# Head 0 of an attention block takes its row tiles in another order, with every engine's queue in that head written out

## The chip, the cores and the metric

The kernel runs on one core of a Trainium2 chip. The metric is the device time of one execution in microseconds; lower is better.

## What is computed

One block over x of 1024 tokens by 256 channels: a layer norm, then 16 heads of causal attention with 128 dimensions each and a small quantised linear layer beside them, both added to x. Cut to what matters:

```python
xn = _layernorm(x)
q, k, v = (xn @ Wq), (xn @ Wk), (xn @ Wv)            # 16 heads of 128
q, k = rmsnorm(q, q_rms_w), rmsnorm(k, k_rms_w)
scores = q k^T / sqrt(128) - distance * slope[head]   # causal
y = rmsnorm(softmax(scores) @ v, subln_w)
x = x + y @ Wproj + quantise_fp8(xn / s) @ (w8 * ws) * s
```

## The kernel before

The kernel is written engine by engine: each of the blocks for SyncE, GpSimd, TensorE, ScalarE and VectorE is one queue in a fixed order, and semaphores tie them together. `over_heads` (L220) calls each engine's `head(h, ...)` for heads 0 and 1 with plain numbers, for 2 to 13 in a loop, and again with numbers for 14 and 15. What is matrix work is done in three products: every float32 operand is split into a rounded high part and a low part, and `product` (L505) multiplies high by high, low by high and high by low.

The 1024 tokens are eight row tiles of 128; two neighbours are a pair (0 to 3). For each head and tile, `project` (L543) makes q, k and v of one tile as six products of 384 columns into one PSUM bank, `copy_qkv` (L772) moves them on ScalarE to a place that `stage_of` names, `square_qk` squares a pair, `mean_squares` (VectorE) sums it, `norm_qk` (GpSimd, L399) takes the reciprocal root and scales q and k with `scale_qk` (L231). In head 0 VectorE scales instead (`norm_first`). `transpose_qk` turns a pair, `qk_hi` (ScalarE) and `qk_lo` (VectorE) split it, `split_v` (GpSimd) splits v.

A row tile i of a head then goes through `score` (i + 1 tiles of 128 keys), `mask` (VectorE adds the bias and takes the row maximum), `exps` (ScalarE), `transpose_probs` (TensorE), `probs_hi` (ScalarE) and `probs_lo` (VectorE). The order of the row tiles is ORDER = 7, 0, 6, 1, 5, 2, 4, 3 in every head. `attend` sums the first four tiles (group 0) in the head itself and the other four in the next. The projections of head h + 1 lie between the row tiles of head h. So in head 0 the queues also hold head 1's projections, norms and transposes, the weights of head 2 (`split_w`) and VectorE's decoding of the 8-bit weights in eight steps (`decode_w8`), which end in `wb_ready`.

Ahead of head 0 lie the loads, the layer norm, 24 warm-up products of TensorE, the transposes of the normalised x (four calls, each waiting for four tiles), ten more warm-ups, the eight projections of head 0 and two of head 1, and the transposes of head 0's q and k. The places for copied projections are two buffers in turn, except for pairs 2 and 3 of head 0, which use halves of `bias` and `probs`. A copy into a used place waits for the norm and the v split of the pair before.

## Time and profile before

| | us |
|---|---|
| median of 3 runs | 534.56 |
| lowest and highest | 532.73 to 536.16 |
| the profiled execution | 534.62 |
| its span, first to last instruction | 532.6 |
| TensorE busy | 512.6 |
| VectorE busy | 436.2 |
| ScalarE busy | 376.9 |
| GpSimd busy | 344.4 |

The times of an engine are from one profiled execution. Matmuls are pipelined, so the next one starts before the one ahead ends: the difference of two starts is what a matmul costs in a row of its kind, and its own duration is what a reader of its result waits. "Idle before" is the time in which the engine did nothing, with the instruction that ended it.

### The profile page before, as it was taken

To read this page: it belongs to the slowest core of one execution; us is meant where nothing else is said; L and a number is where in the kernel's file an instruction comes from. 1 tells how busy PE (TensorE), PEld (TensorE's weight loads), DVE (VectorE), ACT (ScalarE), POOL (GpSimd) and SP (SyncE) were. 2 spreads that over 40 slices of the span, in tenths; PEclk is the share of its full clock that TensorE was granted. 3 is DMA by queue.
4 is the path that set the end of the run, shared out by engine and by line. 5 is a ranking of instruction groups with operands and counts; after the bars stand their busy time and mean duration, and the time that the engine had idled before them with its cause. 6 is when DMAs were issued, how large, how long until landed. Compare 5 with 4: busy or idle time off the path is not lost. (4 is left out here: it accounts for less than half of the span.)

```text
span 532.6 us, 11964 instructions
## 1 busy us (share of the span) xinstructions
PE 512.6 (96%) x3348; PEld 467.0 (88%) x3348; DVE 436.2 (82%) x1061; ACT 376.9 (71%) x887; POOL 344.4 (65%) x491
## 2 busy tenths in 40 slices
PE   8869899999999999999999999999999999999886
PEld 3858699999989999998999999899999999999775
DVE  5768788888898888888888888988888897988973
ACT  2658568676876878677687868678786767869550
POOL 4658387684858668584877848585785848567121
PEclk9999899999999999999999999999999999999998
DMA  5200100001010100101010010101001000000002
GB/s 153 70 1 2 39 1 22 20 2 41 2 40 0 33 7 0 39 0 39 0 39 0 0 39 0 39 0 39 0 0 39 0 10 0 11 1 1 2 0 79
DMA packets 18614, 10.82 MB, mean 20 GB/s; under 512 B 2208, under 2 KB 18592, under 8 KB 18592
## 3 DMA queue, kind: packets, MB, share of 16 engines
q1 hardware_dynamic: 17600, 10.49, 6.7%
q8 instruction: 10, 0.16, 0.1%
q10 hardware_dynamic: 992, 0.07, 0.1%
q14 instruction: 12, 0.10, 0.1%
HBM read 9.51 MB, written 1.05 MB: 20 GB/s over the span
## 5 line engine op out<-in xcount | busy, mean ns | idle before, releaser
L781 ACT ACTIVATE stage<-qkv_ps 128x384 f32<-128x384 f32 x119 | 58.6, 492 | 88.6 <-PE qkv_ps L509 88.6
L973 DVE TENSOR_TENSOR pT_lo<-pT_ps,pT_hi 128x384 fp32r<-128x384 f32 (+1 forms) x192 | 100.6, 552 | 16.0 <-ACT pT_hi L809 15.9
L809 ACT ACTIVATE pT_hi<-pT_ps 128x384 fp32r<-128x384 f32 (+1 forms) x192 | 86.5, 485 | 31.0 <-PE pT_ps L588 31.0
L801 ACT ACTIVATE probs<-probs,neg_max 128x1024 f32<-128x1024 f32 (+7 forms) x128 | 99.1, 775 | 8.4 <-DVE neg_max L964 7.7
L588 PE MATMUL pT_ps<-ident,probs 128*128 128x128 f32 x576 | 86.2, 277 | 5.6 <-ACT probs L801 4.7
L507 PE MATMUL qkv_ps<-w_hi,xT_hi 128*128 128x384 f32 x242 | 87.2, 360 | 0.7 <-DVE xT_lo L1050 0.7
L588 PEld LDWEIGHTS pT_ps<-ident,probs 128*128 128x128 f32 x576 | 66.7, 141 | 18.0 <-ACT probs L801 6.7
L509 PE MATMUL qkv_ps<-w_hi,xT_lo 128*128 128x384 f32 x242 | 81.5, 337 | 0.0
L508 PE MATMUL qkv_ps<-w_lo,xT_hi 128*128 128x384 f32 x242 | 81.3, 336 | 0.0
L403 POOL TENSOR_TENSOR qk_r<-qk_ms,minus_half 128x4 f32<-128x4 f32 x64 | 65.4, 1022 | 21.2 <-DVE qk_ms L938 19.5
L507 PE MATMUL yT_ps<-pT_hi,v_hi 128*128 128x256 f32 (+1 forms) x224 | 73.7, 329 | 0.4 <-DVE pT_lo L973 0.4
L509 PE MATMUL yT_ps<-pT_hi,v_lo 128*128 128x256 f32 (+1 forms) x224 | 72.5, 324 | 0.0
L508 PE MATMUL yT_ps<-pT_lo,v_hi 128*128 128x256 f32 (+1 forms) x224 | 72.3, 323 | 0.0
L964 DVE CUSTOM_DVE_ANT_0 probs<-score_big,bias 128x1024 f32<-128x1024 f32 (+1 forms) x64 | 64.9, 1013 | 2.3 <-PE score_big L509 2.3
L233 POOL TENSOR_TENSOR qk_n<-stage,qk_r 128x512 f32<-128x512 f32 x60 | 62.4, 1040 | 5.7 <-POOL qk_r L403 1.9
L507 PE MATMUL score_big<-kT_hi,qT_hi 128*128 128x512 f32 (+2 forms) x128 | 50.9, 398 | 3.9 <-DVE kT_lo L947 3.9
L935 DVE TENSOR_REDUCE qk_ms<-squares 128x4 f32<-128x512 f32 x62 | 42.4, 683 | 14.1 <-ACT squares L788 13.0
L420 POOL TENSOR_TENSOR v_lo<-stage,v_hi 128x256 fp32r<-128x256 f32 x62 | 46.0, 741 | 9.4 <-POOL v_hi L417 0.5
L507 PEld LDWEIGHTS qkv_ps<-w_hi,xT_hi 128*128 128x128 f32 x242 | 45.9, 190 | 3.6 <-ACT stage L781 2.2
L443 POOL TENSOR_TENSOR y_r<-y_ms,minus_half 128x4 f32<-128x4 f32 x32 | 32.7, 1021 | 22.7 <-DVE y_ms L999 14.9
L508 PEld LDWEIGHTS qkv_ps<-w_lo,xT_hi 128*128 128x128 f32 x242 | 45.7, 189 | 0.0
L509 PE MATMUL score_big<-kT_hi,qT_lo 128*128 128x512 f32 (+2 forms) x128 | 45.6, 356 | 0.0
...
## 6 DMA issues: line engine op xcount, KB each, us to landing
...
q_col<-in_q_w ACTq DMA_DIRECT2D x1, 0.5 KB, 3.0
```

What stands on the lines that cost most here:

```text
L233: eng.tensor_tensor(qk_n[:, k % 2], stage_of(h, k)[:, :, 0:2 * D].rearrange("p t (a d) -> p t a d", d=D), qk_r[:, k % 2, :].rearrange("p ( ...
L403: pool.tensor_tensor(qk_r[:, k % 2, :], qk_ms[:, k % 2, :], minus_half[:, 0:4], ALU.pow).then_inc(qk_r_ready, 1)
L420: pool.tensor_tensor(v_lo[:, par, 2 * k:2 * k + 2, :], v, v_hi[:, par, 2 * k:2 * k + 2, :].bitcast(f32), ALU.subtract).then_inc(v_split, 1)
L507: pe.matmul(dst, a_hi, b_hi, start=start, stop=False)
L508: pe.matmul(dst, a_hi, b_lo, start=False, stop=False)
L509: return pe.matmul(dst, a_lo, b_hi, start=False, stop=stop)
L588: last = pe.transpose(ps[:, (j - a) * P:(j - a + 1) * P], probs[:, s % 2, j * P:(j + 1) * P], ident[:, :])
L781: act.activation(stage_of(h, k // 2)[:, k % 2, :], qkv_bank(h, k)[:, 0:3 * D], ACT.Copy).then_inc(qkv_read, 1)
L801: act.activation(probs[:, s % 2, 0:(i + 1) * P], probs[:, s % 2, 0:(i + 1) * P], ACT.Exp, bias=neg_max[:, par, s:s + 1], scale=-1.0, accum ...
L809: act.activation(pT_hi[g][:, a:b, r * P:(r + 1) * P], pT_ps[(CHUNK0[s] + k) % 2][:, 0:(b - a) * P].rearrange("p (j t) -> p j t", t=P), ACT ...
L964: dve.tensor_tensor_reduce(out=probs[:, s % 2, 0:w], in0=ps[:, at:at + w], in1=bias[:, par, (NT - 1 - i) * P:(NT - 1 - i) * P + w], scale= ...
L973: dve.tensor_tensor(pT_lo[g][:, a:b, r * P:(r + 1) * P], pT_ps[(CHUNK0[s] + k) % 2][:, 0:(b - a) * P].rearrange("p (j t) -> p j t", t=P), ...
```

## The change

- **Order.** Head 0 takes its row tiles as 1, 7, 0, 6, 3, 5, 2, 4; all other heads keep ORDER. The first four are the same group. Row tile 1 is scored into the `misc` bank and needs pair 0 only; each score of head 0 waits for the low part of its own pair instead of for all four.
- **Places.** Pairs 2 to 5 (2 and 3 of head 0, 0 and 1 of head 1) get rooms of their own, in `bias_more` and `early_room`; the latter is shared with y_blocks, w8T, xqT, x_u, x_m and the statistics, which gives those two added waits (`part_y`, the copy of w8T). `probs` is no longer used for a projection, so the second mask of head 0 doesn't wait for the splits of v. Head 1's last projection goes to the other bank, and head 1's first transposes wait for all its copies.
- **Queues.** Every engine but SyncE has a `first_head` with the order in head 0 written out. Pairs 1 and 3 of head 0 are scaled on GpSimd, 0 and 2 on VectorE. The low part of head 0's weights is made on GpSimd instead of VectorE. GpSimd splits head 2's weights and most of v later, after head 1's first norm. TensorE transposes x tile by tile as tiles come, starts a projection when the first half of the contraction is there, and has two more of head 1's projections ahead of the first big score. The last decoding step is one of its own, and head 1's first score goes ahead of the transposes of the 8-bit weights.

The diff, cut to its core. The rest follows from it: `order(h)`, `chunks(h, s)` and `chunk0(h, s)` take the places of ORDER, CHUNKS and CHUNK0 everywhere, and `head` on each engine calls `first_head` and returns where h is 0.

```diff
     ORDER = [7, 0, 6, 1, 5, 2, 4, 3]
+    FIRST_ORDER = [1, 7, 0, 6, 3, 5, 2, 4]
     GROUPS = [sorted(ORDER[:4], reverse=True), sorted(ORDER[4:], reverse=True)]
     RANK = {i: (g, GROUPS[g].index(i)) for g in range(2) for i in GROUPS[g]}
-    CHUNKS = [[(j, min(j + 4, i + 1)) for j in range(0, i + 1, 4)] for i in ORDER]
-    CHUNK0 = [sum(len(c) for c in CHUNKS[:s]) for s in range(NT + 1)]
-    CPH = CHUNK0[NT]
+    def order(h):
+        return FIRST_ORDER if isinstance(h, int) and h == 0 else ORDER
+    def chunks(h, s):
+        i = order(h)[s]
+        return [(j, min(j + 4, i + 1)) for j in range(0, i + 1, 4)]
...
@@ -111,7 +124,11 @@
         yT_hi = sb("yT_hi", [P, 2, 4 * P], f32r)
         yT_lo = sb("yT_lo", [P, 2, 4 * P], f32r)
         y_sq = sb("y_sq", [P, 2, 4 * P])
-        y_blocks = sb("y_blocks", [P, 4 * P])
+        early_room = sb("early_room", [P, 12 * P])
+        y_blocks = early_room[:, 0:4 * P]
+        x_u, x_m = early_room[:, 4 * P:6 * P], early_room[:, 6 * P:8 * P]
+        w8T = early_room[:, 8 * P:10 * P].bitcast(bf16).rearrange("p (k c) -> p k c", k=KT)
+        xqT = early_room[:, 10 * P:11 * P].bitcast(bf16).rearrange("p (k t) -> p k t", k=KT)
         y_part = sb("y_part", [P, 16])
         y_pair = sb("y_pair", [P, 4, 2, 4], f32r)
...
@@ -255,9 +269,10 @@
         def stage_of(h, k):
-            if isinstance(h, int) and h == 0 and k >= 2:
-                room = bias[:, 1, :] if k == 2 else probs[:, 1, :]
-                return room[:, 0:6 * D].rearrange("p (t n) -> p t n", t=2)
+            if isinstance(h, int) and 2 <= NPAIR * h + k < 6:
+                if h == 0:
+                    return bias_more[:, T + (k - 2) * 6 * D:T + (k - 1) * 6 * D].rearrange("p (t n) -> p t n", t=2)
+                return early_room[:, k * 6 * D:(k + 1) * 6 * D].rearrange("p (t n) -> p t n", t=2)
             return stage[:, k % 2]
...
@@ -289,9 +304,11 @@
         def is_last(h):
             return isinstance(h, int) and h == H - 1
-        def score_at(i):
+        def score_at(h, i):
             w = (i + 1) * P
+            if isinstance(h, int) and h == 0 and i == 1:
+                return misc, 0, [(0, w)]
...
             for n in range(2):
                 at = slice(n * NT // 2, (n + 1) * NT // 2)
+                if n == 1:
+                    pool.wait_ge(w_hi_done, 1)
+                    pool.tensor_tensor(w_lo[:, 0], w_raw[:, 0], w_hi[:, 0].bitcast(f32), ALU.subtract).then_inc(w_split, 1)
                 pool.wait_ge(var_ready, n + 1)
                 pool.tensor_tensor(rstd[:, at], rstd[:, at], minus_half[:, at], ALU.pow).then_inc(rstd_ready, 1)
...
+                if isinstance(h, int) and h == 0 and k not in POOL_NORMS:
                     return
                 pool.wait_ge(qk_r_ready, n + 1)
+                if isinstance(h, int) and n <= NPAIR:
+                    past(pool, qk_normed, n)
                 past(pool, qkT_ready, n - 1)
                 scale_qk(pool, h, k)
...
@@ -459,16 +481,36 @@
             split_w(1, 1)
             norm_qk(0, 0)
             norm_qk(0, 1)
-            split_v(0, 0, 0)
             norm_qk(0, 2)
             norm_qk(0, 3)
-            for k in (1, 2, 3):
-                split_v(0, 0, k)
+            split_v(0, 0, 0)
+            split_v(0, 0, 1)
+            norm_qk(1, 0)
             pool.wait_ge(small_loaded, 80)
             pool.wait_ge(xT_read, 2 * KT)
+            split_v(0, 0, 2)
+            split_v(0, 0, 3)
+            split_w(2, 0)
+            def first_head():
+                split_v(1, 1, 0)
+                norm_qk(1, 1)
+                norm_qk(1, 2)
+                norm_qk(1, 3)
+                split_wp(0, 0)
+                split_v(1, 1, 1)
+                split_v(1, 1, 2)
+                split_v(1, 1, 3)
+                pool.wait_ge(ffn_scaled, 1)
+                clip_x(0)
             def head(h, par, tile, after):
                 first, last = isinstance(h, int) and h == 0, is_last(h)
+                if first:
...
-                past(pe, qkv_read, NT * h + k - (1 if isinstance(h, int) and (h == 0 or h == 1 and 1 <= k <= 6) else 0))
+                past(pe, qkv_read, NT * h + k - (1 if isinstance(h, int) and h <= 1 else 0))
                 if k == 0 and not (isinstance(h, int) and h <= 1):
                     pe.wait_ge(misc_read, misc_done(h - 2, "proj1a" if not (isinstance(h, int) and h == 2) else "qkT2"))
                 for kt in range(KT):
+                    if isinstance(h, int) and h == 0 and k % 4 == 0:
+                        pe.wait_ge(xT_read, KT * (k // 4) + kt + 1)
...
-                i, n = ORDER[s], NT * h + s
-                if s == 0:
+                i, n = order(h)[s], NT * h + s
+                if isinstance(h, int) and h == 0:
+                    pe.wait_ge(misc_read, misc_done(-1, f"qkT{i // 2}"))
+                elif s == 0:
                     pe.wait_ge(misc_read, misc_done(h - 1, "qkT3"))
-                past(pe, scores_masked, n - 1)
-                ps, at, parts = score_at(i)
+                past(pe, scores_masked, n if isinstance(h, int) and (h, s) == (1, 0) else n - 1)
+                ps, at, parts = score_at(h, i)
...
-            def transpose_x(n):
-                half, kt = n // KT, n % KT
-                pe.wait_ge(xn_ready, 4 * half + 4)
+            def transpose_x(half):
                 for t in range(4):
-                    last = pe.transpose(xT_bank(n)[:, t * P:(t + 1) * P],
-                                        bias_xn(4 * half + t)[:, kt * P:(kt + 1) * P], ident[:, :])
-                last.then_inc(xT_ready, 1)
+                    pe.wait_ge(xn_ready, 4 * half + t + 1)
+                    for kt in range(KT):
+                        last = pe.transpose(xT_bank(half * KT + kt)[:, t * P:(t + 1) * P],
+                                            bias_xn(4 * half + t)[:, kt * P:(kt + 1) * P], ident[:, :])
+                        if t == 3:
+                            last.then_inc(xT_ready, 1)
             transpose_x(0)
+            warm(KEEP_WARM)
+            project(0, 0, 0)
+            project(0, 0, 1)
             transpose_x(1)
-            warm(KEEP_WARM)
-            for k in range(NT):
-                if k % 4 == 0:
-                    pe.wait_ge(xT_read, KT * (k // 4 + 1))
-                project(0, 0, k)
-                if k == 1:
-                    transpose_x(2)
-                    transpose_x(3)
-                if k == NT - 1:
-                    transpose_qk(0, 0, 0, -1)
-                    transpose_qk(0, 0, 1, -1)
+            project(0, 0, 2)
+            project(0, 0, 3)
+            project(0, 0, 4)
+            project(0, 0, 5)
+            project(0, 0, 6)
+            project(0, 0, 7)
             project(1, 1, 0)
+            transpose_qk(0, 0, 0, -1)
+            transpose_qk(0, 0, 1, -1)
+            project(1, 1, 1)
             transpose_qk(0, 0, 2, -1)
-            project(1, 1, 1)
+            score(0, 0, 0)
             transpose_qk(0, 0, 3, -1)
-            score(0, 0, 0)
             project(1, 1, 2)
+            project(1, 1, 3)
...
+            def first_head():
+                transpose_probs(0, 0)
+                score(0, 0, 1)
+                project(1, 1, 4)
+                project(1, 1, 5)
+                score(0, 0, 2)
+                score(0, 0, 3)
+                transpose_probs(0, 1)
+                project(1, 1, 6)
+                score(0, 0, 4)
+                transpose_probs(0, 2)
+                score(0, 0, 5)
+                transpose_probs(0, 3)
+                project(1, 1, 7)
+                transpose_qk(1, 1, 0, 0)
+                transpose_probs(0, 4)
+                score(0, 0, 6)
+                score(0, 0, 7)
+                transpose_probs(0, 5)
+                transpose_qk(1, 1, 1, 0)
+                transpose_qk(1, 1, 2, 0)
+                attend(0, 0, 0, 0)
+                transpose_probs(0, 6)
+                transpose_qk(1, 1, 3, 0)
+                attend(0, 0, 0, 1)
+                transpose_probs(0, 7)
+                score(1, 1, 0)
+                transpose_w8()
...
                 act.wait_ge(qkv_ready, n + 1)
-                if k % 2 == 0 and not (isinstance(h, int) and h == 0):
-                    last = k // 2 + 1 if isinstance(h, int) and h == 1 and k <= 2 else pair - 1
+                if k % 2 == 0 and not (isinstance(h, int) and pair < 6):
+                    last = pair - 5 if isinstance(h, int) and h == 1 else pair - 1
...
@@ -847,26 +930,72 @@
             round_xT(0)
             round_xT(1)
-            for k in range(NT):
-                copy_qkv(0, k)
-                if k == 1:
-                    round_xT(2)
-                    round_xT(3)
-                if k % 2:
-                    square_qk(0, k // 2)
             act.wait_ge(const_ready, 3)
+            make_bias(0, 0)
+            copy_qkv(0, 0)
+            copy_qkv(0, 1)
+            round_xT(2)
+            round_xT(3)
+            copy_qkv(0, 2)
+            square_qk(0, 0)
+            copy_qkv(0, 3)
+            copy_qkv(0, 4)
+            square_qk(0, 1)
+            copy_qkv(0, 5)
+            copy_qkv(0, 6)
+            square_qk(0, 2)
+            copy_qkv(0, 7)
+            square_qk(0, 3)
             act.wait_ge(wq_col_ready, 1)
-            for k in range(NPAIR):
-                qk_hi(0, 0, k)
-                if k == 1:
-                    copy_qkv(1, 0)
-                    make_bias(0, 0)
-                if k == 2:
-                    copy_qkv(1, 1)
+            qk_hi(0, 0, 0)
+            copy_qkv(1, 0)
+            copy_qkv(1, 1)
+            qk_hi(0, 0, 1)
+            qk_hi(0, 0, 2)
             square_qk(1, 0)
+            qk_hi(0, 0, 3)
+            exps(0, 0, 0)
+            probs_hi(0, 0)
+            copy_qkv(1, 2)
+            copy_qkv(1, 3)
+            def first_head():
+                copy_qkv(1, 4)
+                exps(0, 0, 1)
+                square_qk(1, 1)
+                probs_hi(0, 1)
+                exps(0, 0, 2)
+                copy_qkv(1, 5)
+                square_qk(1, 2)
+                probs_hi(0, 2)
+                exps(0, 0, 3)
+                copy_qkv(1, 6)
+                exps(0, 0, 4)
+                probs_hi(0, 3)
+                copy_qkv(1, 7)
+                square_qk(1, 3)
+                qk_hi(1, 1, 0)
+                probs_hi(0, 4)
+                exps(0, 0, 5)
+                exps(0, 0, 6)
+                probs_hi(0, 5)
+                qk_hi(1, 1, 1)
+                make_bias(1, 1)
+                exps(0, 0, 7)
+                probs_hi(0, 6)
+                qk_hi(1, 1, 2)
+                qk_hi(1, 1, 3)
+                act.wait_ge(wb_ready, 1)
+                square_y(0, 0)
+                y_hi(0, 0, 0)
             def head(h, par, tile, after):
                 first, last = isinstance(h, int) and h == 0, is_last(h)
+                if first:
+                    first_head()
...
@@ -1067,10 +1207,8 @@
             variances(0)
             normed(0)
             moments(1)
+            split_xT(0)
             variances(1)
-            split_xT(0)
-            dve.wait_ge(w_hi_done, 1)
-            dve.tensor_tensor(w_lo[:, 0], w_raw[:, 0], w_hi[:, 0].bitcast(f32), ALU.subtract).then_inc(w_split, 1)
             split_xT(1)
             normed(1)
...
+                if s == 7:
                     dve.scalar_tensor_tensor(wide, sign, 1.0, mag, ALU.add, ALU.mult).then_inc(wb_ready, 1)
             def norm_first(k):
                 dve.wait_ge(qk_r_ready, k + 1)
                 past(dve, qkT_ready, k - 1)
...
+                link(dve.reciprocal(ffn_s[:, 1:2], ffn_s[:, 0:1]))
+                dve.tensor_tensor(ffn_s[:, 3:4], ffn_s[:, 0:1], ffn_s[:, 2:3], ALU.mult).then_inc(ffn_scaled, 1)
             mean_squares(0, 0)
             mean_squares(0, 1)
             norm_first(0)
             mean_squares(0, 2)
-            norm_first(1)
             mean_squares(0, 3)
+            norm_first(2)
             qk_lo(0, 0, 0)
-            norm_first(2)
-            norm_first(3)
             qk_lo(0, 0, 1)
             qk_lo(0, 0, 2)
+            mask(0, 0, 0)
             qk_lo(0, 0, 3)
-            mask(0, 0, 0)
+            mean_squares(1, 0)
             def add_ffn(h, t):
...
+            def first_head():
+                decode_w8(0)
+                decode_w8(1)
+                mask(0, 0, 1)
+                decode_w8(2)
+                decode_w8(3)
+                probs_lo(0, 0)
+                mean_squares(1, 1)
+                mask(0, 0, 2)
+                mask(0, 0, 3)
+                probs_lo(0, 1)
+                decode_w8(4)
+                probs_lo(0, 2)
+                mask(0, 0, 4)
+                mean_squares(1, 2)
+                decode_w8(5)
+                probs_lo(0, 3)
+                mask(0, 0, 5)
+                mask(0, 0, 6)
+                mean_squares(1, 3)
+                probs_lo(0, 4)
+                qk_lo(1, 1, 0)
+                scale_ffn()
+                mask(0, 0, 7)
+                probs_lo(0, 5)
+                qk_lo(1, 1, 1)
+                decode_w8(6)
+                probs_lo(0, 6)
+                decode_w8(7)
+                qk_lo(1, 1, 2)
+                qk_lo(1, 1, 3)
+                y_lo(0, 0)
+                probs_lo(0, 7)
+                mask(1, 1, 0)
```

## Rows read from the trace of the kernel before

**Rows 1.** TensorE and the others by stretches: stretch, length, busy us (instructions), then granted clock (PEclk).

```profile
0.00:62.00 62.00, 50.89 (x282) 40.65 (x283) 43.60 (x111) 35.45 (x78) 37.16 (x67) 0.97 0.20 57
62.00:94.00 32.00, 31.93 (x216) 29.44 (x215) 26.23 (x64) 24.32 (x57) 23.01 (x32) 1.00 0.06 17
```

**Rows 2.** Waits of TensorE, 0 to 62 us: total, times, longest

```profile
PE score_big L507 <- DVE kT_lo L947: 3.9, 2, 2.2
PE pT_ps L588 <- ACT probs L801: 2.8, 2, 1.9
...
PE score_small L564 <- DVE qk_n L233: 0.8, 1, 0.8
...
PE score_big L564 <- DVE qk_n L233: 0.6, 1, 0.6
```

**Rows 3.** The same, 62 to 503 us

```profile
PE pT_ps L588 <- ACT probs L801: 0.8, 1, 0.8
```

**Rows 4.** The view by stretches again, around two stops of TensorE

```profile
32.00:36.00 4.00, 2.14 (x14) 1.92 (x13) 2.24 (x5) 1.51 (x4) 2.66 (x3) 1.00 0.01 4
58.00:59.00 1.00, 0.60 (x2) 0.51 (x3) 1.00 (x4) 0.83 (x3) 0.00 (x0) 0.74 0.83 239
59.00:60.00 1.00, 1.00 (x4) 0.81 (x3) 0.74 (x2) 0.00 (x0) 0.00 (x0) 0.50 0.12 34
...
61.00:62.00 1.00, 1.00 (x7) 0.87 (x6) 0.00 (x0) 0.00 (x0) 0.00 (x0) 0.56 0.00 0
```

**Rows 5.** Timeline of TensorE: start, busy us, line, operation, count, idle before

```profile
11.02 2.32 PE L651 MATMUL score_big<-ident_b 128*128 128x512 bf16 x10
14.08 0.45 PE L507 MATMUL qkv_ps<-w_hi,xT_hi 128*128 128x384 f32 x1 [0.74 <-DVE xT_lo L1050]
...
15.24 0.33 PE L507 MATMUL yT_ps<-w_hi,xT_hi 128*128 128x384 f32 x1
...
16.28 0.60 PE L662 MATMUL misc<-ident,bias 128*128 128x128 f32 x4
...
30.94 0.50 PE L507 MATMUL score_big<-kT_hi,qT_hi 128*128 128x512 f32 x1 [1.69 <-DVE kT_lo L947]
...
35.78 1.09 PE L588 MATMUL pT_ps<-ident,probs 128*128 128x128 f32 x8 [1.86 <-ACT probs L801]
...
58.40 0.75 PE L507 MATMUL score_big<-kT_hi,qT_hi 128*128 128x512 f32 x1 [2.18 <-DVE kT_lo L947]
...
62.48 0.39 PE L507 MATMUL qkv_ps<-w_hi,xT_hi 128*128 128x384 f32 x1
```

**Rows 6.** Timeline of GpSimd

```profile
16.35 1.83 POOL L382 TENSOR_TENSOR w_lo<-w_raw,w_hi 128x768 fp32r<-128x768 f32 x1
...
21.59 1.39 POOL L403 TENSOR_TENSOR qk_r<-qk_ms,minus_half 128x4 f32<-128x4 f32 x1 [0.88 <-DVE qk_ms L938]
...
25.83 1.01 POOL L403 TENSOR_TENSOR qk_r<-qk_ms,minus_half 128x4 f32<-128x4 f32 x1 [0.21 <-DVE qk_ms L938]
...
41.90 1.04 POOL L233 TENSOR_TENSOR qk_n<-stage,qk_r 128x512 f32<-128x512 f32 x1
```

**Rows 7.** Timeline of VectorE

```profile
12.48 0.95 DVE L1073 TENSOR_TENSOR w_lo<-w_raw,w_hi 128x768 fp32r<-128x768 f32 x1
...
21.42 0.69 DVE L233 TENSOR_TENSOR qk_n<-stage,qk_r 128x512 f32<-128x512 f32 x1
...
23.50 1.25 DVE L233 TENSOR_TENSOR qk_n<-stage,qk_r 128x512 f32<-128x512 f32 x1
...
33.22 1.23 DVE L964 CUSTOM_DVE_ANT_0 probs<-score_big,bias 128x1024 f32<-128x1024 f32 x1 [2.33 <-PE score_big L509]
...
55.73 1.00 DVE L1113 TENSOR_TENSOR y_sq<-y_sq,wb 128x512 f32<-128x512 f32 x1
56.77 0.85 DVE L1114 SCALAR_TENSOR_TENSOR wb<-y_sq 128x512 bf16<-128x512 f32 x1
```

**Rows 8.** Timeline of ScalarE

```profile
15.43 0.49 ACT L781 ACTIVATE stage<-qkv_ps 128x384 f32<-128x384 f32 x1 [3.56 <-PE qkv_ps L509]
```

108 lines of the change are left out of this document (67 added, 41 removed).

## The prediction, made before the changed kernel ran

> **What bounds the kernel now.** I read the busy time by stretches first. From 62 us to 94 us TensorE is busy 31.93 of 32 us, in the first 62 us only 50.89 [rows 1]. The waits of TensorE say the same for the rest: between 62 and 503 us its largest wait is 0.8 us [rows 3]. So heads 1 to 14 are a solid block of matmuls and only the two ends have air. The change touches head 0 and the projections of head 1, all of it before TensorE begins head 2's first projection, and nothing behind that point runs in another order. The question is therefore one number: when does that projection start? Before, it starts at 62.48 us [rows 5], and whatever it moves forward the end moves forward too, as long as head 1 stays a solid block.
>
> In front of it the reader is to see three losses.
> - The start: TensorE's first real product begins at 14.08 us [rows 5].
> - Stops after that: 3.9 us for k's low part (kT_lo) in two stops, 2.8 us for probabilities in two, 0.8 and 0.6 us for normalised q and k [rows 2]. The sum is 8.1 us.
> - A slow stretch: before the score at 58.40 TensorE waits for kT_lo (the longest stop on its list of waits, 2.2 us [rows 2]), and then the granted clock is 0.74, 0.50 (twice) and 0.56 in the four microseconds from 58 to 62 [rows 4], that is 1.2 GHz for most of them. Lost: 0.26 + 0.50 + 0.50 + 0.44 = 1.7 us.
>
> From 14.08 to 62.48 are 48.4 us; less 8.1 and 1.7 this leaves 38.6 us of work. That is the same work after the change: 16 projections, 8 + 8 groups of transposes, nine score tiles (and head 1's second), the 36 tiles of probabilities, one half attention. As a cross-check: six matmuls of 384 columns take 16.28 - 15.24 = 1.04 us, so 0.173 us each, or 0.45 ns a column, and eight transposes take 1.09 us with their drain of some 0.24, or 0.107 each [rows 5]. About 61,000 columns at 0.45 ns are 27.5 us, 76 transposes at 0.107 us are 8.1 us; the rest of the 38.6 us is the change between kinds and the drain at a stop.
>
> **The change part by part.**
>
> *The start.* The low part of head 0's weights goes from VectorE (0.95 us, at 12.48 [rows 7]) to GpSimd, where the same operation on head 1's weights takes 1.83 us [rows 6]. Its input is ready when ScalarE has rounded the high part, at 10.3 us, so it ends at about 12.2. On GpSimd the second reciprocal root is queued behind it; VectorE now asks for that at about 12.6, so the root waits for nothing and is merely 0.6 us later than before, while VectorE, which has lost 0.95 us of work, reaches the second normalisation at 13.8 against 13.95. VectorE's low part of x is now first needed for one half of the contraction only, and is there at 12.2; the second at 13.3. The transposes of x start at about 9.9 us when the 24 warm-up products end, finish at about 10.8, ten warm-ups (2.32 us [rows 5]) follow, and the first projection starts at 13.15 instead of 14.08. Gain 0.9 us. The bounds: 12.2, if the warm-ups were to end sooner (they don't depend on data), and 14.1, if the GpSimd subtraction took twice as long. The second group of transposes then starts right after two projections. Squares, sums and roots of the first three pairs come no earlier, though: ScalarE does each square one copy later than before, so these 0.9 us are not passed on to them.
>
> *The norms.* Pairs 1 and 3 are scaled on GpSimd for 1.04 us [rows 6] instead of on VectorE for 0.69 to 1.25 us [rows 7]. VectorE's queue gets shorter, GpSimd's longer by 2 us, and its order changes: the splits of v, head 2's weights (2.75 us) and the splits of head 1's v are put behind head 1's first norm. Walking the queues with these durations gives normalised pair 1 at 23.95, pair 2 at 25.8, pair 3 at 27.4. TensorE has eight projections done at 22.45, one of head 1's and the first two transposes at 24.4, another projection at 25.45. Then it stops 0.4 us for pair 2, 0.25 for the low part of pair 0 (the small score needs only this one, which is what the order 1, 7, 0, 6 brings) and 0.45 for pair 3: 1.1 us in place of 0.8 + 0.6 + 1.7 us.
>
> *The big score.* Row tile 7 is scored at about 30.25 instead of 30.94 [rows 5], but with two more projections (2.1 us), a small score and its transposes already done. The copies of these projections wait for no buffer, since pairs 2 to 5 have rooms of their own. While mask (1.23 us), exponentials (1.15 us and a read of the sum) run [rows 7, 8], TensorE has two projections and one short score in hand and 1.4 us of row tile 6: the stop of 1.86 us at 35.78 goes, and so does the next of 0.95 (together the 2.8 us of [rows 2]).
>
> *The middle of the head.* What is late next are the handovers between ScalarE and VectorE. The fourth set of transposes (row tile 6) needs exponentials that follow the copies of tile 0's transposes, which wait for VectorE behind the mask of tile 6: 0.45 us. Head 1's first transposes go into the bank of the projection just before them; they wait for its copy, 0.19 us after the last product and 0.49 us long [rows 8]: 0.75 us. The transposes of tile 5 wait for exponentials and then for the low part of tile 3: 0.4 + 0.4 us. Head 1's fourth transposes wait for the low parts of pair 1, which stand behind a mask and two low parts: 0.8 us.
>
> *The score of head 1.* It needs the low part of pair 3, behind the last two steps of the decoding (1.00 and 0.85 us [rows 7]), one low part of probabilities and pair 2's. With the gaps between instructions, after pair 1's low part, that is 1.05 + 0.45 + 0.85 + 2 x 0.75 = 3.85 us on VectorE, against 0.45 + 1.8 + 0.6 us on TensorE: a stop of 1.0 us instead of 2.2. The bounds are 0 and 2.2 us. I take 1.0; at that length no row shows a fall of the clock (the stop of 1.86 us ahead of 35.78 [rows 5] left it at 1.00 [rows 4]), so the 1.7 us of the slow stretch are saved whole.
>
> *Ports.* VectorE and GpSimd disturb each other. The root on GpSimd takes 1.39 us beside a VectorE product of two SBUF operands, and 1.01 us later on [rows 6]; the same VectorE product takes 0.69 us, and 1.25 beside a GpSimd subtraction [rows 7]. I have put 0.45 us for this into the three norm stops. The Trainium skill, SBUF — State Buffer, section "Who interferes with whom", says that the first to issue holds the shared pair for its whole instruction and the other blocks fully, and counts VectorE's two-port modes, such as the decoding's tensor_scalar steps, among those concerned. By that rule, GpSimd being busy without a break from 27 to 54 us, six decoding steps would wait up to 1 us each.
>
> *The rest* costs nothing: the bias made earlier lies in ScalarE's idle time while head 0 is projected; buffers that share room (w8T, xqT and the x tiles with pairs 4 and 5) are written only in head 1, and their added waits are for pairs that GpSimd has finished by 51 us; the loads of weights hang on splits that are not late.
>
> **The sum.** New start of head 2's first projection: 13.15 + 38.6 + stops of (1.1 + 0.45 + 0.75 + 0.8 + 0.8 + 1.0 = 4.9) = 56.65 us, against 62.48. Gain 5.8 us: 0.9 start, 3.2 stops, 1.7 clock. The queue walk itself, instruction by instruction, ended at 56.1, so 5.8 is the careful side. The profiled execution took 534.62 us beside a span of 532.6; the median of three is 534.56, so both are the same here: 534.6 - 5.8 = 528.8 us, with a span near 526.8.
>
> **Rivals.**
> 1. *The VectorE queue becomes the bound of head 0.* VectorE has hardly a pause there, in a fixed order in which decoding and sums stand between masks and low parts. If each of six decoding steps is held by GpSimd for 0.4 to 0.6 us (1.25 - 0.69 is 0.56 [rows 7]), 2.4 to 3.6 us come back into the stops and the gain is 2.2 to 3.4 us: about 531.8 us. For it: GpSimd has hardly a pause after 27 us. Against: most of this delay would have to fall on the steps TensorE waits for. This is also what the skill's rule of the shared port would give. Chance 0.23.
> 2. *The handovers hide better than walked.* If the stops in the middle overlap with slack that I count double (the walk's 56.1, or the 2 us of middle stops gone), the gain is 7 to 9 us: 526.6 us. Against: the decode-and-low-part chain ahead of head 1's score is serial. Chance 0.15.
> 3. *It does not shorten anything:* the stop before head 1's score stays over 2 us because normalised pair 3 of head 1 comes late from GpSimd (it waits for the transposes of pair 1), the clock drops as at 58.40 and the 1.7 us return: gain 5.8 - 1.2 - 1.7 = 2.9, or with rival 1 nothing. Time about 531.7 us, chance 0.11.
> 4. *Slower than before:* a fall of the clock early. The three norm stops at 25 to 28 us lie 1 us apart; if the chip answers them with 1.2 GHz until head 0 is through, 26 us, then at the half microsecond that each microsecond of it cost in [rows 4] 13 us are lost: 534.6 - 5.8 + 13 = 541.8 us. It eats the gain from 12 us of half clock on, and makes the kernel slower by over 1% from 22 us on. Against: before, stops of 0.8, 0.6, 1.69 and 1.86 us within 12 us left the clock at 1.00 [rows 2, 4, 5]. Chance 0.06.
>
> **How the numbers follow.** The forecast (gain 4.5 to 7) holds 0.45. A change under 1% (5.35 us) can't be told from none by a measurement of this kernel. The forecast's span is cut by that bound: of its 0.45, 0.35 lie above it. With rival 2 faster has 0.50; within 1% has 0.44, which is rivals 1 and 3 and the rest of the forecast; slower has rival 4's 0.06. The range of 8 in 10 reaches from rival 2's far end (gain 9) to a gain of 1.5: 525.6 to 533.0 us.
>
> **What would show it.** Right: first projection near 13.1; score of row tile 7 near 30.2 with four of head 1's projections behind it; stops after 13 us that sum to about 5 us, none of 2 us; granted clock 1.00 from 13 us on; head 2's first projection at 56 to 57; the rest as before. Wrong: a stop of over 2 us before head 1's score with a clock of 0.5 behind it; decoding steps on VectorE of 0.8 us and more; new waits of TensorE between 60 and 100 us, where head 1 would have to lose what head 0 gained.

## The result

The changed kernel takes 525.99 us (median of four, 525.42 to 526.85), the kernel before 534.92 beside it: ratio 0.9849, 95% interval 0.9818 to 0.9879. A second set of runs gave 526.79 us and a ratio of 0.9847 (0.9823 to 0.9872). The forecast was 528.8 us, range 525.6 to 533.0. The sign, the place and the three parts (start, stops, clock) were right; the gain is 8.9 us in the first set and 7.7 in the second, against 5.8.

The stretches of the profile of after (stretch, length, busy us with instructions, then granted clock), cut where head 2's first projection now starts:

```profile
0.00:54.68 54.68, 49.56 (x288) 39.59 (x288) 41.55 (x110) 36.09 (x79) 39.79 (x68) 1.00 0.23 65
54.68:86.68 32.00, 32.00 (x214) 29.88 (x214) 26.24 (x64) 23.74 (x56) 24.66 (x36) 1.00 0.06 18
```

Beside [rows 1]: the same 32 us of solid block follow, but from 54.68 us on instead of 62.48. TensorE's waits, first up to 60 us and then to 495 us (total, times, longest):

```profile
PE pT_ps L634 <- ACT probs L883: 0.7, 2, 0.4
PE yT_ps L608 <- ACT stage L863: 0.6, 1, 0.6
PE pT_ps L634 <- DVE pT_lo L1110: 0.5, 2, 0.3
PE misc L608 <- DVE kT_lo L1086: 0.4, 1, 0.4
...
PE score_big L549 <- DVE kT_lo L1086: 0.3, 1, 0.3
```

```profile
PE yT_ps L549 <- DVE pT_lo L1110: 0.4, 1, 0.4
```

The 8.1 us of [rows 2] in six stops have become 2.5 us in seven, none over 0.6; from 55 to 495 us there is hardly a wait, as in [rows 3]. The marks of the forecast in TensorE's timeline of after (start, busy us, operation, idle before):

```profile
9.01 1.41 PE L708 MATMUL pT_ps<-ident,bias 128*128 128x128 f32 x8 [0.39 <-DVE bias L1183]
10.26 2.32 PE L697 MATMUL score_big<-ident_b 128*128 128x512 bf16 x10
12.23 0.53 PE L549 MATMUL qkv_ps<-w_hi,xT_hi 128*128 128x384 f32 x1
...
24.92 0.34 PE L551 MATMUL yT_ps<-w_hi,xT_lo 128*128 128x384 f32 x1
25.39 0.66 PE L608 MATMUL score_big<-ident,qk_n 128*128 128x128 f32 x4
...
29.48 0.48 PE L549 MATMUL score_big<-kT_hi,qT_hi 128*128 128x512 f32 x1
...
40.99 0.34 PE L551 MATMUL yT_ps<-w_hi,xT_lo 128*128 128x384 f32 x1
41.91 0.66 PE L608 MATMUL yT_ps<-ident,qk_n 128*128 128x128 f32 x4 [0.58 <-ACT stage L863]
...
44.80 0.66 PE L634 MATMUL pT_ps<-ident,probs 128*128 128x128 f32 x4 [0.41 <-ACT probs L883]
45.72 0.44 PE L634 MATMUL pT_ps<-ident,probs 128*128 128x128 f32 x2 [0.26 <-DVE pT_lo L1110]
...
49.37 0.66 PE L608 MATMUL misc<-ident,qk_n 128*128 128x128 f32 x4 [0.44 <-DVE kT_lo L1086]
...
52.61 0.50 PE L549 MATMUL score_big<-kT_hi,qT_hi 128*128 128x512 f32 x1 [0.31 <-DVE kT_lo L1086]
...
54.68 0.39 PE L549 MATMUL qkv_ps<-w_hi,xT_hi 128*128 128x384 f32 x1
```

Against [rows 5]: the first projection starts at 12.23 instead of 14.08, the score of row tile 7 at 29.48 instead of 30.94 with four of head 1's projections done instead of two, head 1's first score at 52.61 instead of 58.40 and at full clock (its first product takes 0.50 us, not 0.75), head 2's first projection at 54.68.

So 7.8 us were won up to there in this pair of traces; the span fell by 8.8, from 532.6 to 523.8. The other 1.0 us can't be credited to the change. From head 2's first projection on TensorE runs the same 3061 products in both. All but the last sixty take 454.1 us in before and 454.7 in after, and between 453.8 and 455.1 in all fourteen traces, whatever the kernel. The last sixty take 11.1 us where the clock fell among them (before, twice, and one execution of after) and 9.5 us in the other eleven, 1.6 us less: near the end both kernels have the same stops, and the clock fell there in one execution and not in the other. Granted clock of before, of the same kernel profiled once more, and of after profiled once more:

```profile
520.00:521.00 1.00, 1.00 (x4) 0.72 (x3) 0.26 (x1) 0.00 (x0) 0.63 (x1) 0.50 0.00 0
```

```profile
59.00:60.00 1.00, 1.00 (x4) 0.74 (x3) 0.57 (x1) 0.00 (x0) 0.00 (x0) 0.50 0.00 0
...
520.00:521.00 1.00, 1.00 (x3) 0.74 (x3) 0.45 (x2) 0.00 (x0) 0.44 (x1) 0.50 0.00 0
```

```profile
512.00:513.00 1.00, 1.00 (x5) 0.90 (x5) 0.38 (x2) 0.00 (x0) 0.43 (x1) 0.57 0.00 0
513.00:514.00 1.00, 1.00 (x3) 0.72 (x3) 0.28 (x1) 0.00 (x0) 0.61 (x1) 0.50 0.00 0
```

### The profile page after: what moved, and what is told of

It is laid out like the page before. It is cut to its first block and busy times, and to the rows that moved or that the text cites. A ratio compares the mean times of both kernels' runs of the same rounds, so it can differ in the third digit from the quotient of the medians.

```text
span 523.8 us, 11974 instructions
## 1 busy us (share of the span) xinstructions
PE 509.9 (97%) x3348; PEld 465.2 (89%) x3348; DVE 433.6 (83%) x1058; ACT 377.3 (72%) x887; POOL 349.5 (67%) x494
## 3 DMA queue, kind: packets, MB, share of 16 engines
HBM read 9.51 MB, written 1.05 MB: 20 GB/s over the span
## 5 line engine op out<-in xcount | busy, mean ns | idle before, releaser
L863 ACT ACTIVATE stage<-qkv_ps 128x384 f32<-128x384 f32 x116 | 57.2, 493 | 88.1 <-PE qkv_ps L551 88.1
L1110 DVE TENSOR_TENSOR pT_lo<-pT_ps,pT_hi 128x384 fp32r<-128x384 f32 (+2 forms) x192 | 100.8, 552 | 11.9 <-ACT pT_hi L891 11.7
L891 ACT ACTIVATE pT_hi<-pT_ps 128x384 fp32r<-128x384 f32 (+2 forms) x192 | 86.8, 486 | 28.8 <-PE pT_ps L634 28.7
L883 ACT ACTIVATE probs<-probs,neg_max 128x256 f32<-128x256 f32 (+7 forms) x128 | 99.1, 776 | 3.2 <-DVE neg_max L1101 2.3
L1074 DVE TENSOR_REDUCE qk_ms<-squares 128x4 f32<-128x512 f32 x62 | 42.4, 684 | 13.5 <-ACT squares L870 13.5
L442 POOL TENSOR_TENSOR v_lo<-stage,v_hi 128x256 fp32r<-128x256 f32 x60 | 44.4, 739 | 8.7
```

The costliest lines, as they stand in the source:

```text
L442: pool.tensor_tensor(v_lo[:, par, 2 * k:2 * k + 2, :], v, v_hi[:, par, 2 * k:2 * k + 2, :].bitcast(f32), ALU.subtract).then_inc(v_split, 1)
L863: act.activation(stage_of(h, k // 2)[:, k % 2, :], qkv_bank(h, k)[:, 0:3 * D], ACT.Copy).then_inc(qkv_read, 1)
L883: act.activation(probs[:, s % 2, 0:(i + 1) * P], probs[:, s % 2, 0:(i + 1) * P], ACT.Exp, bias=neg_max[:, par, s:s + 1], scale=-1.0, accum ...
L891: act.activation(pT_hi[g][:, a:b, r * P:(r + 1) * P], pT_ps[(chunk0(h, s) + k) % 2][:, 0:(b - a) * P].rearrange("p (j t) -> p j t", t=P), ...
L1110: dve.tensor_tensor(pT_lo[g][:, a:b, r * P:(r + 1) * P], pT_ps[(chunk0(h, s) + k) % 2][:, 0:(b - a) * P].rearrange("p (j t) -> p j t", t=P ...
```

## The experiments

The ruler of most runs is the distance from TensorE's first projection to head 2's first projection, read from each trace, since everything the change does to the queues lies in it and the start is taken out. "At full clock" is this distance less half a microsecond for each microsecond at half clock in it; that takes the slow stretches as pure loss, which is an upper bound, because other engines catch up meanwhile. Each ratio is against executions of the kernel before made beside that run, whose medians were 534.92, 534.27, 533.65 and 534.45 us in the four sets, so it is the ratios that compare across rows, not the times.

| run | first projection | head 2's | distance | at full clock | time, us | ratio to before (95%) |
|---|---|---|---|---|---|---|
| before | 14.08 | 62.48 | 48.40 | 46.7 | 534.92 | |
| before, again | 13.90 | 62.32 | 48.42 | 46.7 | 535.81 (one) | |
| before, stop filled | 14.11 | 61.92 | 47.81 | 46.1 | 533.08 | 0.9976 (0.9957 to 0.9994) |
| before, new start | 12.34 | 61.20 | 48.86 | 47.2 | 532.62 | 0.9980 (0.9959 to 1.0001) |
| before, new order | 13.97 | 62.35 | 48.38 | 45.4 | 532.78 | 0.9963 (0.9946 to 0.9980) |
| before, new rooms | 13.93 | 62.98 | 49.05 | 46.1 | 534.07 | 0.9998 (0.9983 to 1.0012) |
| after | 12.23 | 54.68 | 42.45 | 42.4 | 525.99 | 0.9849 (0.9818 to 0.9879) |
| after, again | 12.71 | 54.95 | 42.24 | 42.2 | 526.79 | 0.9847 (0.9823 to 0.9872) |
| after, old start | 13.94 | 56.05 | 42.11 | 42.1 | 527.33 | 0.9890 (0.9851 to 0.9928) |
| after, norms on VectorE | 12.58 | 55.24 | 42.66 | 42.7 | 526.62 | 0.9870 (0.9829 to 0.9911) |
| after, GpSimd's old-like order | 12.39 | 55.58 | 43.19 | 43.2 | 527.49 | 0.9892 (0.9845 to 0.9938) |
| after, rooms shared | 12.87 | 61.85 | 48.98 | 49.0 | 534.23 | 1.0009 (0.9988 to 1.0030) |
| after, old tile order | 12.20 | 66.07 | 53.87 | 50.5 | 537.33 | 1.0065 (1.0042 to 1.0087) |
| after, three more stops | 12.19 | 54.44 | 42.25 | 42.2 | 526.17 | 0.9871 (0.9826 to 0.9916) |

### The stop filled with idle products

```diff
                     elif not last:
+                        if first:
+                            pe.wait_ge(scores_masked, NT - 1)
+                            warm(9)
                         score(h + 1, 1 - par, 0)
```

> The kernel before, with nine idle products of 512 columns (about 2.1 us at full clock) put into the 2.2 us stop ahead of head 1's first score, so that TensorE is never still there; no stop gets shorter. If the slow stretch behind that stop was the clock's answer to it, the clock stays at 1.00 from 56 to 62 us, head 2's first projection starts 1.7 us earlier than 62.48 (60.8 us) and the time falls by 0.3%. If the clock falls for another reason, the stretch stays and the time is the same or up to 1 us longer, for products that run past the stop.

The clock stayed at 1.00 from 58 to 62 us, as my theory had it, but it fell elsewhere, behind the stops of 1.69 and 1.86 us that had left it alone in [rows 4]:

```profile
37.00:38.00 1.00, 1.00 (x3) 0.76 (x3) 0.77 (x2) 0.61 (x2) 0.00 (x0) 0.50 0.00 0
...
40.00:41.00 1.00, 1.00 (x7) 0.89 (x5) 0.97 (x4) 0.60 (x2) 0.00 (x0) 0.91 0.00 0
58.00:59.00 1.00, 1.00 (x6) 0.33 (x4) 1.00 (x3) 0.65 (x3) 0.75 (x2) 1.00 0.56 168
60.00:61.00 1.00, 1.00 (x6) 0.78 (x5) 0.77 (x2) 0.00 (x0) 0.00 (x0) 1.00 0.03 9
```

Head 2's first projection came 0.56 us earlier, not 1.7, because 1.7 us were lost at 37 to 41 instead. Over ten executions the time is 0.24% lower (1.3 us), and (1 - mean granted clock) x span is 1.8 us on average against 3.1 in the 25 executions of the kernel before beside them. So over many executions the stop does cost slow stretches, and filling it saves them; and a stop of 1.7 to 1.9 us can bring one as well: the sentence of the forecast that no row shows it was true of one execution only.

### The kernel before once more

> The kernel before once more, for its clock. If slow stretches of TensorE depend on the phase in which a stop falls, this execution has them at other places than 58 to 62 and 519 to 523 us (after the stops of 30.9 or 35.8 us, or none); its stops have the same lengths as before up to 0.2 us, but for the stretch in which the clock fell. If the 2.2 us stop alone brings it, the clock falls at 58 again.

The same places as in the first profile (rows above: 58 to 62, and 519 to 523 us), stops of the same length. The first 24 warm-ups took the same 7.96 us in both executions, and the falls of the clock came out alike. In the run with new rooms the first 24 took 7.25 us, and the clock fell both behind the 1.83 us stop and behind the 2.21 us one. That the warm-ups' length sets it isn't shown: with the new start they took 7.33 us, and the clock fell behind the 2.19 us stop and not behind the 1.83 us one. The run with new rooms:

```profile
37.00:38.00 1.00, 1.00 (x4) 0.76 (x3) 0.95 (x2) 0.45 (x1) 0.00 (x0) 0.50 0.00 0
...
61.00:62.00 1.00, 1.00 (x6) 0.87 (x5) 0.00 (x0) 0.00 (x0) 0.00 (x0) 0.50 0.00 0
```

### The start alone, and all but the start

```diff
+                if n == 1:
+                    pool.wait_ge(w_hi_done, 1)
+                    pool.tensor_tensor(w_lo[:, 0], w_raw[:, 0], w_hi[:, 0].bitcast(f32), ALU.subtract).then_inc(w_split, 1)
                 pool.wait_ge(var_ready, n + 1)
...
             moments(1)
-            variances(1)
             split_xT(0)
-            dve.wait_ge(w_hi_done, 1)
-            dve.tensor_tensor(w_lo[:, 0], w_raw[:, 0], w_hi[:, 0].bitcast(f32), ALU.subtract).then_inc(w_split, 1)
+            variances(1)
             split_xT(1)
```

and the new `transpose_x` and the wait by halves with it; the second run takes the same lines out of the changed kernel.

> The kernel before with only the start of the change: weights' low part on GpSimd, x transposed tile by tile, the projection waiting by halves. My theory: the first projection starts at 12.2 to 13.2 us instead of 14.08, the eight projections end about as much earlier, but the squares and roots follow ScalarE's old order and head 0 passes on some of it; head 2's first projection 0.9 to 1.8 us earlier and the time 0.2 to 0.3% lower. The rival, that stops behind it swallow the lead because the norms aren't earlier, expects the first projection early and head 2's at 62.0 or later, the time unchanged.

> The changed kernel with the old start (low part of the weights on VectorE, x transposed in four calls ahead of the warm-ups, projection waiting for both halves). My theory: the first projection back at about 14.0 us, head 2's first at 56 to 56.5 instead of 54.68, so the time is 1.2 to 1.9 us above the changed kernel's, ratio to before 0.987 to 0.989. If the start gives nothing that lasts, head 2's first projection stays within 0.4 us of 54.68.

Put into the kernel before, the start moves the first projection by 1.74 us and head 2's by 1.28; taken out of the changed kernel, by 1.71 and 1.37. In times it is 0.20% (1.1 us) and 0.4% (2.2 us) by the ratios; the first interval reaches 1, and those of the second pair overlap, so the times alone don't tell it and the traces carry the reading. The lead lasts in both pairs, with 0.3 to 0.5 us of it swallowed.

### The order alone, and all but the order

```diff
-    FIRST_ORDER = [1, 7, 0, 6, 3, 5, 2, 4]
+    FIRST_ORDER = [7, 0, 6, 1, 5, 2, 4, 3]
...
-            score(0, 0, 0)
             transpose_qk(0, 0, 3, -1)
+            score(0, 0, 0)
...
-            mask(0, 0, 0)
             qk_lo(0, 0, 3)
+            mask(0, 0, 0)
```

The run also takes out what belongs to the small first score: its place in `misc` and its wait for pair 0 alone. The queues stay as they were written for the new order.

> The changed kernel with head 0's row tiles in the old order 7, 0, 6, 1, 5, 2, 4, 3, the first score behind all four pairs' low parts; rooms, norms and queues stay new. My theory: the order's worth is the small score and its transposes ahead of row tile 7 and long tiles next to short ones; without it TensorE stops about 1.3 us for the first exponentials as the next tile is tile 0, and again around tile 6, so head 2's first projection comes 1 to 3 us later than 54.68. The rival, that rooms and queues alone carry the gain, expects it within 0.5 us.

Far more than either theory: head 2's first projection at 66.07 us, 11.4 later, and a kernel slower than before. TensorE's stops in it:

```profile
29.11 0.69 PE L547 MATMUL score_big<-kT_hi,qT_hi 128*128 128x512 f32 x1 [1.71 <-DVE kT_lo L1084]
...
46.55 0.42 PE L632 MATMUL pT_ps<-ident,probs 128*128 128x128 f32 x2 [0.90 <-ACT probs L881]
...
49.51 0.95 PE L606 MATMUL yT_ps<-ident,qk_n 128*128 128x128 f32 x4 [1.49 <-ACT stage L861]
...
55.85 0.52 PE L632 MATMUL pT_ps<-ident,probs 128*128 128x128 f32 x3 [1.85 <-DVE pT_lo L1108]
...
64.00 0.50 PE L547 MATMUL score_big<-kT_hi,qT_hi 128*128 128x512 f32 x1 [1.30 <-DVE kT_lo L1084]
```

The clock fell twice (29 to 33 and 49 to 54 us), 3.4 us together; the other 8 us are stops. The first tile is now the longest one, and behind it ScalarE's queue, written for a short one, holds the copies of head 1's projections: ScalarE waits 5.18 us for the mask, and copies head 1's pair 1 after it only.

```profile
33.38 1.15 ACT L881 ACTIVATE probs<-probs,neg_max 128x1024 f32<-128x1024 f32 x1 [5.18 <-DVE neg_max L1099]
...
36.34 0.50 ACT L861 ACTIVATE early_room<-qkv_ps 128x384 f32<-128x384 f32 x1
```

The reverse, the new order in the old queues:

```diff
             transpose_qk(0, 0, 2, -1)
+            score(0, 0, 0)
             project(1, 1, 1)
             transpose_qk(0, 0, 3, -1)
-            score(0, 0, 0)
...
             qk_lo(0, 0, 2)
-            qk_lo(0, 0, 3)
             mask(0, 0, 0)
+            qk_lo(0, 0, 3)
```

> The kernel before with only the order of head 0's row tiles changed to 1, 7, 0, 6, 3, 5, 2, 4, the small first score and its mask ahead of pair 3's; rooms and queues stay, so tile 7 is masked into the half of probs that pair 3 still holds and waits for all four v splits. My theory, after the run with the old order in the new queues came out 11.4 us late: order and queues only work together. Here tile 7's mask waits for the last v split of head 0 (30.9 us), which it reaches at about 33 anyway, TensorE has only one projection beside that chain, and head 2's first projection comes between 61.0 and 64 us (62.48 before). The rival, that the order by itself carries the gain, expects it at 59 or earlier.

62.35 us, within my theory's span, with the clock down twice (36 to 40 and 59 to 64 us). The time is 0.37% lower (2.0 us by the ratio), so the order alone carries about a quarter of the gain. The stop for the small first score shrinks from 1.69 to 0.64 us, but the next one, for tile 7's exponentials, grows from 1.86 to 2.23:

```profile
31.21 0.50 PE L522 MATMUL score_big<-kT_hi,qT_hi 128*128 128x512 f32 x1 [0.64 <-DVE kT_lo L964]
...
35.64 1.91 PE L605 MATMUL pT_ps<-ident,probs 128*128 128x128 f32 x8 [2.23 <-ACT probs L818]
```

### The rooms alone, and all but the rooms

> The kernel before with only the rooms of their own for pairs 2 to 5 and the waits that follow from them. My theory: rooms by themselves are worth under 0.5 us, because in the old queues ScalarE reaches head 1's first copies when the places are already free; head 2's first projection at 62.0 to 62.5 with a slow stretch like before, time unchanged. The rival, that rooms are worth the 6.3 us that sharing them cost in the new queues, expects 56 to 58 us.

Ratio 0.9998. In the old queues nothing waits for a room: in the trace of before, wherever ScalarE is idle ahead of a copy of head 1's projections (0.30, 0.81, 0.55 and 0.39 us), TensorE's product ends the wait. In the new ones the rooms' removal needs GpSimd's splits between the norms again (pair 3's copy would otherwise never be let in), so that order is a run of its own:

```diff
+            split_v(1, 1, 0)
             split_w(2, 0)
...
-                split_v(1, 1, 0)
                 norm_qk(1, 1)
+                split_v(1, 1, 1)
                 norm_qk(1, 2)
+                split_v(1, 1, 2)
                 norm_qk(1, 3)
+                split_v(1, 1, 3)
                 split_wp(0, 0)
```

> The changed kernel with GpSimd's queue of head 0 nearly as before: head 1's v splits between its norms again, and the output weights last; rooms stay new. My theory: norm of head 1's pair 2 comes 1.1 us and pair 3 up to 2.2 us later than now (43.8 and 47.8 us); pair 3's transposes wait at 49.4 already, so at most 0.7 us is lost, head 2's first projection at 54.7 to 55.4. If GpSimd's order is what shortens the head, it comes after 56.

Head 2's first projection at 55.58 us, 0.2 us past my span; by distance 0.7 to 1.0 us are lost, a little more than the 0.7 I had allowed. Then the two rooms of head 1 on top; those of head 0's pairs 2 and 3 stay:

```diff
-            if isinstance(h, int) and 2 <= NPAIR * h + k < 6:
+            if isinstance(h, int) and 2 <= NPAIR * h + k < 4:
...
-                if k % 2 == 0 and not (isinstance(h, int) and pair < 6):
-                    last = pair - 5 if isinstance(h, int) and h == 1 else pair - 1
+                if k % 2 == 0 and not (isinstance(h, int) and pair < 4):
+                    last = (k // 2 + 1 if k <= 2 else pair - 1) if isinstance(h, int) and h == 1 else pair - 1
```

> As the run with GpSimd's old-like order, and head 1's pairs 0 and 1 share the two staging rooms again, so each copy waits for norm and v split of the pair two before (head 0's pairs 2 and 3 keep rooms in the enlarged bias). My theory: head 1's first copy waits for head 0's first v split, which GpSimd ends at about 27.9 us instead of 24.3, and ScalarE holds pair 1's high part behind it; row tile 7's score starts 3 us later than 29.48 and head 2's first projection is at 57.5 to 60. The rival, that rooms are worth nothing, expects the same time as the run with GpSimd's old-like order.

61.85 us: 6.3 later than with that order and rooms (5.8 by distance), more than I expected, and all of the change's gain is gone (ratio 1.0009). ScalarE shows where: head 1's first copy waits until GpSimd has split head 0's first v (28.31 us), and its fifth until head 1's first v is split (39.49 us), which stands behind head 0's last two splits in GpSimd's queue; tile 7's exponentials stand behind that copy:

```profile
28.39 0.49 ACT L861 ACTIVATE stage<-qkv_ps 128x384 f32<-128x384 f32 x1 [3.60 <-issue]
...
39.58 0.49 ACT L861 ACTIVATE stage<-qkv_ps 128x384 f32<-128x384 f32 x1 [5.45 <-POOL v_lo L440]
39.97 1.14 ACT L881 ACTIVATE probs<-probs,neg_max 128x1024 f32<-128x1024 f32 x1
```

TensorE stops 3.28 us for those exponentials. The clock stayed at 1.00 through the longest stop of all runs:

```profile
39.00:40.00 1.00, 0.00 (x0) 0.00 (x0) 0.00 (x0) 0.42 (x2) 1.00 (x2) 1.00 0.00 0
...
41.00:42.00 1.00, 0.75 (x7) 0.75 (x8) 0.25 (x1) 0.77 (x4) 1.00 (x1) 1.00 0.00 0
```

### The norms, and three more stops

```diff
-        POOL_NORMS = (1, 3)
+        POOL_NORMS = ()
```

with `norm_first(1)` and `norm_first(3)` on VectorE.

> The changed kernel with all four norms of head 0 scaled on VectorE as before. My theory from the walk: VectorE takes 0.69 to 1.25 us each for two more of them, between sums and low parts; pair 1 comes no later, pair 3 about 0.5 us earlier, the low parts of pairs 1 and 2 about 0.7 us later. Row tile 7's score starts within 0.5 us of 29.48 and head 2's first projection within 0.5 us of 54.68. If the split between GpSimd and VectorE is what keeps VectorE's chain short, head 2's projection is 1 us or more later.

55.24 us, just outside my 0.5 us, but the start was 0.35 us late in it; by distance 0.2 to 0.4 us more: who scales pairs 1 and 3 hardly matters.

```diff
-                transpose_qk(1, 1, 0, 0)
                 transpose_probs(0, 4)
+                transpose_qk(1, 1, 0, 0)
...
-                qk_hi(1, 1, 0)
                 probs_hi(0, 4)
                 exps(0, 0, 5)
+                qk_hi(1, 1, 0)
...
                 qk_lo(1, 1, 0)
-                scale_ffn()
                 mask(0, 0, 7)
                 probs_lo(0, 5)
                 qk_lo(1, 1, 1)
-                decode_w8(6)
                 probs_lo(0, 6)
-                decode_w8(7)
+                decode_w8(6)
                 qk_lo(1, 1, 2)
                 qk_lo(1, 1, 3)
+                decode_w8(7)
+                scale_ffn()
```

> The changed kernel with three of the remaining stops taken away: the last decoding step and the ffn scale go behind head 1's pair 3 on VectorE, the step before them behind one more low part, and the transposes of row tile 3 go ahead of head 1's first transposes, on ScalarE with their high part and tile 5's exponentials. My theory: the stops of 0.3 us ahead of head 1's score, 0.44 ahead of pair 3's transposes, 0.41 and 0.26 at tile 5 go or halve; head 2's first projection at 53.5 to 54.2 instead of 54.68, the time 0.5 to 1.2 us below the changed kernel's, about what such a run can just tell.

54.44 us and 526.17: not told apart from the changed kernel, and short of the 0.5 to 1.2 us expected. The stop for pair 3's transposes went and that for pair 0's became one of 0.42 us for tile 3's; the rest came back one handover on, ahead of tile 5's second part and of head 1's score, and the idle time sums to 2.6 us against 2.5:

```profile
45.53 0.44 PE L634 MATMUL pT_ps<-ident,probs 128*128 128x128 f32 x2 [0.81 <-DVE pT_lo L1110]
...
52.37 0.50 PE L549 MATMUL score_big<-kT_hi,qT_hi 128*128 128x512 f32 x1 [0.80 <-DVE kT_lo L1086]
```

The score still waits for pair 3's low part, and VectorE stood still 0.86 us for tile 2's high part on ScalarE before it got there.

### The changed kernel once more

> The changed kernel once more, beside the other runs. Its first projection at 12.2 to 12.6 us whatever the first 24 warm-ups take (6.65 to 7.95 us in the traces so far), head 2's first at 54.6 to 55.3, no slow stretch before 500 us, perhaps one of up to 1.7 us in the last 20 us; ratio to before 0.983 to 0.988.

As expected but for the first projection, 12.71, 0.1 us past my span. It isn't the first 24 warm-ups, though they took 7.80 us instead of 6.65: the ten later ones began at 10.48 and would have let it start at 12.45. It is GpSimd's subtraction for head 0's weights, which ended at 12.66 us, because the weights had come later and ScalarE rounded them at 9.92 instead of 9.36 us. ScalarE and GpSimd in this execution, and TensorE in the run with shared rooms, where this wait stands in the list:

```profile
9.92 0.84 ACT L924 ACTIVATE w_hi<-w_raw 128x768 fp32r<-128x768 f32 x1 [5.02 <-DMA w_raw<-in_wv]
10.84 1.82 POOL L390 TENSOR_TENSOR w_lo<-w_raw,w_hi 128x768 fp32r<-128x768 f32 x1 [2.47 <-ACT w_hi L924]
```

```profile
12.87 0.44 PE L547 MATMUL qkv_ps<-w_hi,xT_hi 128*128 128x384 f32 x1 [0.52 <-POOL w_lo L388]
```

The clock was down at 512 to 516 us (rows above).

## Why the prediction was right, and where it was short

**The bound and the place** held: TensorE is a solid block behind head 2's first projection in both kernels ([rows 1, 3] and their like of after), 454.1 and 454.7 us up to the last sixty products.

**The start** was put at 0.9 us and is worth 1.2 to 1.9: 14.08 to 12.23 in the first pair, 1.7 in the two runs that move it alone, of which 1.3 to 1.4 reach head 2. The step that was off is the chain of transposes and warm-ups on TensorE. I let the transposes begin at 9.9 us, when the 24 warm-ups had ended in [rows 5]'s execution, and added the ten later ones with their full 2.32 us. In after the transposes began at 9.01 as soon as the first tile was there, the ten at 10.26 instead of 10.8, and the first projection starts 1.97 us after they do, not 2.32. Where the 24 took longest, 7.94 us, the ten still began at 10.61. So in the eight traces with the new start the first projection comes at the later of two times: 1.97 us after the ten have begun, or 0.05 us after GpSimd's subtraction, which I had named as the lower bound, 12.2 us (it ended at 12.11 in after and at 12.81 at the latest). That gives 12.2 to 12.9 us.

**The stops** were put at 4.9 us in place of 8.1, so 3.2 won; here lies the other half of the miss (1.05 us, beside 0.95 in the start), and it is one of bookkeeping. The walk of the queues gave stops as distances between starts; the 8.1 us of [rows 2] are idle times behind the modelled end of a product, each 0.17 us shorter. The rows of after show both: the product at 40.99 costs 0.173 us, so from 41.16 to 41.91 are 0.75 us of stop, listed as 0.58; and between 24.92 and 25.39 lies a stop of 0.3 us that the list of waits doesn't have. By starts before has 9.5 us: the six stops with 0.17 us more each, and one of 0.3 ahead of 53.31 that isn't listed. The 38.6 us of work in the forecast therefore held 1.4 us of stops. The whole distance closes in this measure. Between the two marks both kernels run the same 245 products (80 transposes among them, not the 76 of the forecast), which take 36.1 us at what each costs in a row of its kind.

| us, by starts | before | after |
|---|---|---|
| products | 36.1 | 36.1 |
| stops over 0.15 us | 9.5 | 4.9 |
| half clock | 1.7 | 0 |
| smaller pieces | 1.2 | 1.4 |
| distance | 48.4 | 42.4 |

(The sums are off by the rounding.) So 4.6 us of stops were won, not 3.2. That after's stops sum to the 4.9 us forecast is partly luck: head 1's first transposes took the 0.75 us walked, but the stop ahead of head 1's score was put at 1.0 and is 0.5, and that for pair 1's low parts at 0.8 and is 0.6, while tile 5's transposes were put at 0.8 and took 1.0, and other small ones nobody walked fill the rest.

The last decoding steps ahead of that score took 0.69 and 0.68 us, not the 1.00 and 0.85 of [rows 7]. VectorE and GpSimd still meet there, but now VectorE comes first and GpSimd is the one that takes longer: its subtraction beside the first took 1.21 us, where the same one takes 0.73 in before, and its cast beside the second 0.90, where 0.40 is usual.

```profile
49.31 1.21 POOL L416 TENSOR_TENSOR wp_lo<-wp_raw,wp_hi 128x256 fp32r<-128x256 f32 x1
50.46 0.90 POOL L439 CAST v_hi<-early_room 128x256 fp32r<-128x256 f32 x1
```

**The clock** was put at 1.7 us, and the stretch at 58 to 62 is gone. But the reason given, that a stop under 1.9 us leaves the clock alone, is refuted by the filled run and by the one with new rooms. Over all executions, (1 - mean granted clock) x span is 3.2 us on average for 57 of the kernel before and 1.0 us for eight of after. So about 2 of the 7.7 to 8.9 us are clock, through fewer and shorter stops, not through one. In six traces, two of after and one each of the four runs close to it, no stop behind the first projection is over 0.81 us, and the clock didn't fall before 500 us.

**Rival 1**, VectorE held by GpSimd in the decoding, didn't happen. The seven decoding steps behind the first take 0.41 to 0.85 us each; the four that took 0.42 us each before take 0.43, 0.42, 0.85 and 0.41 now, so one was held. All eight together take 4.3 us instead of 5.0. Four of them:

```profile
32.40 0.42 DVE L1243 TENSOR_SCALAR y_sq<-y_sq 128x512 f32<-128x512 int32 x1
32.85 0.85 DVE L1245 TENSOR_SCALAR y_sq<-y_sq 128x512 int32<-128x512 int32 x1
...
49.23 0.69 DVE L1251 TENSOR_TENSOR y_sq<-y_sq,wb 128x512 f32<-128x512 f32 x1
...
50.42 0.68 DVE L1253 SCALAR_TENSOR_TENSOR wb<-y_sq 128x512 bf16<-128x512 f32 x1
```

The rule in the Trainium skill (SBUF — State Buffer, "Who interferes with whom") says which instructions can block each other, and that the one that issues first holds the shared pair. The trace agrees: the 0.85 us step began 0.17 us after a GpSimd subtraction, and the step at 49.23 began 0.08 us before the one it delayed.

**Rival 2**, handovers that hide better, has the gain in its range of 7 to 9 us, but not by its mechanism: the handovers took in sum what was walked, and the start, the two measures of a stop and the clock near the end made the difference. **Rival 3** is bounded: pair 3 of head 1 is normed at 47.8 us, 1.6 ahead of its transposes. **Rival 4**, a half clock through the whole head, didn't occur in any run; each of the ten falls in the traces' first 66 us cost 1.7 us.

**What no step of the forecast said**, and the runs showed: the parts don't add. In the old kernel start, order and rooms are worth 0.20%, 0.37% and nothing; together with the written-out queues 1.5%. Taken out of the finished whole, by the ratios against 0.985, the start costs 0.4% (within the intervals), GpSimd's order and head 1's rooms together 1.6%, and the tile order 2.2%. That the old order in the new queues falls below the kernel before is shown; which of its stops belong to which queue was not taken apart further. What stays open is the queues' own share: no run writes the queues out for the old tile order, or has order and rooms together in the old queues. So the 2.2% is what it costs to take the order out of queues written for it, and not what the order is worth against the best queues for the old one. That a change under 1% can't be told from none was too careful: ten executions of the filled run, beside 25, told 0.24%.
